# Three tile buffers, one x1 chunk buffer, and the final 1x1 in four whole chunks, in a two-layer convolution kernel on one Trainium2 core

## The reference, cut to what matters

```python
# layer 0; gn is group normalisation with 32 groups of 16 channels
g   = gn(x)
f   = relu(einsum('oc,nchw->nohw', Wc, g) + bc)              # 512 -> 128 channels, 1x1
gk1 = relu(mean(g, axis=(2, 3)) @ Wc.T + bc)                  # gate from the means
xm  = g.reshape(N, C, 3, H // 3, 3, W // 3).max(axis=(3, 5))  # 3x3 grid of maxima
sk  = relu(einsum('oc,nckl->nokl', Wc, xm) + bc)
dynW = relu(Wck applied to (gk1 * Wkk + bkk, sk) + bck)       # a 3x3 kernel of its own for each image
y   = conv3x3(f, dynW) + b_ad                                 # 128 -> 128 channels
x1  = x + einsum('oc,nchw->nohw', Wf, y) + bf                 # the final 1x1, 128 -> 512 channels
# layer 1
out = x1 + conv3x3_grouped(gn(x1), kernels, groups=32)        # 16 -> 16 channels in each group
```

## Time and profile before

| | us |
|---|---|
| median of 3 runs | 4146.16 |
| the profiled execution, its own time | 4137.59 |
| its span | 4135.8 |
| mean granted clock of TensorE | 0.953 |

### The profile page before, as it was taken

How to read it: one execution, slowest core, us unless ns; L and a number is a source line. 1 busy time by engine, 2 the same in 40 slices (tenths; PEclk the granted TensorE clock), 3 DMA queues, 4 the chain that set the end, 5 groups by cost and what they waited for, 6 DMA issues and landing times.

```text
span 4135.8 us, 60434 instructions
## 1 busy us (share of the span) xinstructions
PE 3670.0 (89%) x18688; PEld 2884.0 (70%) x18688; DVE 2569.5 (62%) x5557; ACT 2126.7 (51%) x3559; POOL 960.6 (23%) x1036
## 2 busy tenths in 40 slices
PE   4798998899998889998889988899988899888996
PEld 3676777667777667777667766677766677766774
DVE  5766666666666666666566656666666666666642
ACT  3355555555554555545555555655445555555554
POOL 2022222222212222122222222222222222222223
PEclk9899999999999999999999999999999999999997
DMA  4465655765656756656756557656567566576555
GB/s 91 139 186 154 173 155 148 189 174 162 169 144 153 200 159 167 170 139 168 187 154 171 153 142 196 170 166 163 149 155 191 157 166 166 141 183 179 146 150 123
DMA packets 317590, 666.98 MB, mean 161 GB/s; under 512 B 58863, under 2 KB 288242, under 8 KB 288645
## 3 DMA queue, kind: packets, MB, share of 16 engines
q1 hardware_dynamic: 317317, 663.34, 61.0%
HBM read 355.00 MB, written 308.28 MB: 160 GB/s over the span
## 4 chain that ended last, share of the span: by engine, by line
issue 65%; POOL 20%; PE 9%; DVE 2%; DMA 2%; ACT 1%; POOLq 1%; SPq 0%; DVEq 0%; ACTq 0%
POOL hl L408 19%; PE pb L858 1%; PE pb L860 1%; PE pb L859 1%; DMA big<-x_rows 1%; PE pac L858 1%; POOLq L407 1%; PE pd L858 1%; PE pd L859 1%; PE pd L860 1%; PE pac L859 1%; PE pac L860 1%; DMA out<-big 1%; DVE big L779 1%; DVE x1b L769 0%
## 5 line engine op out<-in xcount | busy, mean ns | idle before, releaser
L408 POOL TENSOR_TENSOR hl<-un,hl 128x384 f16<-128x384 f32 x1024 | 933.2, 911 | 3094.2 <-ACT hl L433 3094.0
L429 ACT ACTIVATE un<-big,b_t,s_t 128x384 f32<-128x384 f32 x1024 | 710.8, 694 | 455.2 <-DMA big<-x_rows 455.2
L858 PE MATMUL pd<-hl,k_h 128*96 128x384 f16 x1536 | 541.1, 352 | 234.9 <-POOL hl L408 234.9
L433 ACT ACTIVATE hl<-un 128x384 f16<-128x384 f32 x1024 | 538.9, 526 | 275.3 <-PE pb L860 183.9
L779 DVE SCALAR_TENSOR_TENSOR big<-pd,kout,big 96x768 f32<-96x768 f32 x256 | 259.2, 1012 | 539.5 <-PE pd L860 539.5
L858 PE MATMUL pb<-fh,dynh 128*128 128x480 f32 (+1 forms) x1440 | 549.6, 382 | 23.8 <-DVE xs L755 23.8
L860 PE MATMUL pb<-fh,dynl 128*128 128x480 f32 (+1 forms) x1440 | 546.5, 379 | 0.0
L859 PE MATMUL pb<-fl,dynh 128*128 128x480 f32 (+1 forms) x1440 | 545.2, 379 | 0.0
L859 PE MATMUL pd<-hl,k_h 128*96 128x384 f16 x1536 | 537.1, 350 | 0.0
L860 PE MATMUL pd<-hl,k_l 128*96 128x384 f16 x1536 | 536.9, 350 | 0.0
L443 ACT ACTIVATE xs<-big,negm 128x480 fp32r<-128x480 f32 (+1 forms) x640 | 401.0, 671 | 227.1 <-PE pac L860 225.0
(11 more groups left out here) (114 smaller groups left out, 5505.0 us busy)
## 6 DMA issues: line engine op xcount, KB each, us to landing
big<-x SPq DMA_DIRECT2D x128, 1152.0 KB, 9.9
x_rows<-x1b SPq DMA_DIRECT2D x128, 1152.0 KB, 6.6
big<-x_rows SPq DMA_DIRECT2D x128, 1152.0 KB, 9.5
out<-big SPq DMA_DIRECT2D x128, 1152.0 KB, 6.4
big<-x_rows SPq DMA_DIRECT2D x256, 192.0 KB, 10.8
x_rows<-mrow SPq DMA_DIRECT2D x64, 96.0 KB, 1.9
big<-kt SPq DMA_DIRECT2D x4, 288.0 KB, 10.8
big<-kt SPq DMA_DIRECT2D x2, 192.0 KB, 11.8
```

Of the source, the lines that this page charges most:

```text
L408: pool.tensor_tensor(hl[:, g % HL_RING, 1, :, 1:W + 1], un[:, g % U_RING], hl[:, g % HL_RING, 0, :, 1:W + 1], ALU.subtract).then_inc(hl_lo, 1)
L429: act.activation(un[:, g % U_RING], t_slot(g // GQ)[:, g % GQ], ACT.Identity, bias=b_t[:, g:g + 1], scale=s_t[:, g:g + 1]).then_inc(u_done, 1)
L433: act.activation(hl[:, g % HL_RING, 0, :, 1:W + 1], un[:, g % U_RING], ACT.Copy).then_inc(hl_hi, 1)
L858: pe.matmul(acc, high_w, high_x, start=start, stop=False)
```

## The change

There are three tile buffers, so chunks 0, 1 and 2 have one each and chunk 3 follows chunk 0. There is one chunk buffer for x1, so chunk c may be filled when chunk c-1 is written and squared. The final 1x1 has a whole chunk of six units in each of rounds 0, 4, 8 and 11. The group means of x1, and their transfers, move from stage D into the next step, between stages A and B; all tile loads stand behind them. The squares and some statistics move to other rounds. Image 1's loads no longer wait for `k_lo`; step 1's `write_means` does.

```diff
-X1_SLOTS = 2
-T_SLOTS = 2
-T_SLOT = [0, 1, 0, 1]
+X1_SLOTS = 1
+T_SLOTS = 3
+T_SLOT = [0, 1, 2, 0]
-C_ROUNDS = 6
-C_PER_ROUND = CUNITS // C_ROUNDS
+C_AT = {0: 0, 4: 1, 8: 2, 11: 3}
-SQUARE_AFTER = {7: 0, 10: 1, 13: 2, 16: 3}
-ROOT_AFTER = 24
-GATES_AFTER = 30
+SQUARE_AFTER = {6: 0, 14: 1, 22: 2, 28: 3}
+ROOT_AFTER = 23
+GATES_AFTER = 28
...
                     sp.wait_ge(max_done, Q)
-                    sp.wait_ge(k_lo, K_PARTS)
...
                 if T_SLOT[c] in T_SLOT[:c]:
                     sp.wait_ge(stored[T_SLOT.index(T_SLOT[c])], written)
                 else:
-                    reached(sp, stored[Q - 1 - T_SLOT[::-1].index(T_SLOT[c])], free)
+                    sp.wait_ge(stored[Q - 1 if c == 0 else c], written)
...
                 if k == 0:
-                    if c < X1_SLOTS:
-                        reached(vec, x1_out[c + X1_SLOTS], n * 16)
-                        reached(vec, sq_done, n * Q)
+                    if c == 0:
+                        reached(vec, x1_out[Q - 1], n * 16)
                     else:
-                        vec.wait_ge(x1_out[c - X1_SLOTS], (n + 1) * 16)
-                        vec.wait_ge(sq_done, n * Q + c - X1_SLOTS + 1)
+                        vec.wait_ge(x1_out[c - 1], (n + 1) * 16)
+                    reached(vec, sq_done, n * Q + c)
...
                 if d:
+                    x1_group_means(n - 1)
                     x1_variances(n - 1)
```

More of the change, by code:

```diff
@@ L68 @@
 PREP_MEANS_AT = 6
+GROUP_MEAN_AFTER = 7
 PREP_VARIANCES_AT = 8
[L70 to L73, removed]
 GROUP_VARIANCE_AFTER = 9
-KERNEL_INPUTS_AFTER = 12
-KERNELS_AFTER = 14
-X_HIGH_AFTER = {26: (0, 1), 28: (2, 3), 30: (4,)}
+PREP_SCALED_AT = 10
+KERNEL_INPUTS_AFTER = 11
+KERNELS_AFTER = 13
+X1_SUMS_AT = 12
+X_HIGH_AFTER = {28: (0, 1), 30: (2, 3), 31: (4,)}
 X_LOW_AT = {13: (0, 1), 14: (2, 3), 15: (4,)}
@@ L304, in load_t @@
             def load_t(n, c):
-                written, free = (n + 1) * 16, n * 16
+                written = (n + 1) * 16
                 above, below = partition_of(0), partition_of(IR - 1)
@@ L333, in step @@
                     store(n - 2, Q - 1)
+                if more:
+                    load_x(n + 1, 1 - odd, 2)
+                    load_x(n + 1, 1 - odd, 3)
                 if d:
@@ L336, in step @@
                         sp.wait_ge(k_lo, K_PARTS)
[L337 to L343, removed]
+                    write_means(n - 1)
+                    for c in range(Q - 1):
+                        load_t(n - 1, c)
                 write_x1(n, 0)
@@ L376, in _ @@
             store(N - 2, Q - 1)
-            for c in range(2):
+            write_means(N - 1)
+            for c in range(Q - 1):
                 load_t(N - 1, c)
[L379 to L382, removed]
+            store(N - 1, 0)
+            load_t(N - 1, Q - 1)
+            for c in range(1, Q):
                 store(N - 1, c)
             for c in range(Q):
-                sp.wait_ge(stored[c], N * 16)
+                sp.wait_ge(stored[c], (N + 1 if c else N) * 16)
         @block.gpsimd
@@ L390, in _ @@
             pool.memset(stage, 0.0).then_inc(bands_zero, 1)
+            for c in range(1, Q):
+                pool.memset(token[:, c:c + 1], 0.0).then_inc(stored[c], 16)
             pool.memset(ind[:, :, :], 1.0).then_inc(pool_const, 1)
@@ L803, in step @@
                         output(n - 1, r)
-                    if r < C_ROUNDS:
-                        for u in range(r * C_PER_ROUND, (r + 1) * C_PER_ROUND):
+                    if r in C_AT:
+                        for u in range(C_AT[r] * OR_, (C_AT[r] + 1) * OR_):
                             residual(n, odd, u)
@@ L818, in step @@
                         x1_means(n)
-                    if r == X1_MEANS_AT:
-                        x1_group_means(n, more)
                     if more:
@@ L846, in _ @@
             images(vec, step)
+            x1_group_means(N - 1)
             x1_variances(N - 1)
@@ L923, in kernel_inputs @@
                     pe.matmul(acc, cent[:, c, :], wcs[:, c, :], start=c == 0, stop=False)
-                pe.matmul(acc, f32(onesr[0:1, 0:GATES]), bcr[0:1, :], start=False, stop=True).then_inc(stat_mm, 1)
+                pe.matmul(acc, f32(onesr[32:33, 0:GATES]), gates[32:33, :], start=False, stop=True).then_inc(stat_mm, 1)
             def dyn_kernels(n):
@@ L959, in step @@
                         d_pair(n - 1, r)
-                    if r < C_ROUNDS:
-                        for u in range(r * C_PER_ROUND, (r + 1) * C_PER_ROUND):
+                    if r in C_AT:
+                        for u in range(C_AT[r] * OR_, (C_AT[r] + 1) * OR_):
                             c_unit(n, u)
-                    if r == GROUP_VARIANCE_AFTER:
+                    if r == PAIRS - 1:
                         x1_group_means(n)
```

21 lines of the change are left out of this document (9 added, 12 removed).

## The result

The changed kernel takes 3792.81 us (median of 4 runs, 3790.61 to 3798.21). The kernel before took 4145.38 in the same comparison; the ratio is 0.9158, with a 95% interval from 0.9133 to 0.9183. The profiled execution of the changed kernel took 3793.06, its span is 3791.3. Against the 4137.59 and 4135.8 of before that is 344.5 less, where the prediction had 375.

A forecast was written before the change was run, and what follows sets the result against it. TensorE was taken as the bound, losing time in stage D to late tile loads and low clock. Sums of 360 and 391 gave a middle of 375: 4137.6 - 375 = 3763, stated as 3765; 8 in 10 from 3712 to 3860.

The forecast's parts named there:

- likeliest case: Whole kernel: the forecast itself, a time of 3715 to 3830 us, chance 0.74.
- first sum: Full steps: waits 7.0, clock 3.1, means 0.5, final 1x1 0.7 make 11.3, less 0.5; 360 with both ends.
- new timetable: Stage D and start of B: issue and landing times; tile load 3 lands at 33 to 35, six us to spare.
- Squares: Stage D, ScalarE, after groups 6, 14, 22 and 28: groups behind them ready 0.5 to 0.9 early; 0.2 us taken.
- rival 1: Stage D: ScalarE late behind its squares, each a us late; 5.5 lost a stage, time 3935, chance 0.11.
- rival 3: Stage D: tile load 3 stays late, half of the loss stays; 5.3 a stage, time 3929, chance 0.04.
- single chunk buffer: Stage D: a single write takes 5.6 us where 12.0 and 9.2 are available; wait taken as 0.
- Step 0: First image: 26 gained against 17.7 for three waits for a write, partly hidden; bounds 8 and 26, 18 taken.
- the 26: Step 0: TensorE's wait of 23.81 for x of image 1 goes and its clock is kept, 26 us gained.
- second count: Stage D counted up from its parts: 65.3, 12.3 less than 77.6; less 0.5, with 25.5 for the ends, 391.
- stage A: Start of each step: 15.2 us, counted as filled, with no change foreseen.
- The last step and the last image: End of run: a stage D's 11.3 - 0.5, and 10.5 less some 3 us for the first tile load, 7.5.

The follow-up runs named there:

- e2: Changed kernel with two tile buffers instead of three, loads 2 and 3 queued behind the writes of chunks 1 and 2: 4293.44 us, ratio 1.0375.
- e7: Against the two-tile-buffer kernel e2: tile load 3 moved ahead of the write of chunk 2 in SyncE's queue: 4121.26 us, ratio 0.9954.
- e3: Changed kernel with chunk 1 of the final 1x1 moved from round 4 to round 1, next to chunk 0: 3908.23 us, ratio 0.944.
- e4: Changed kernel with one scaling of the next image's 1x1 weights moved from round 10 to 11, its small products to round 12: 3752.66 us, ratio 0.9067.
- e5: Changed kernel with the low part of the next image's dynamic kernels made before round 15's output on VectorE: 3663.38 us, ratio 0.8851.
- e10: Changed kernel with the loop over images ended two images earlier and these two steps written out behind it: 3793.83 us, ratio 0.9163.
- e8: The changed kernel measured a second time, unchanged: 3797.18 us, ratio 0.9176.

## Why the prediction was right, and where it was off

The forecast of 3765 stood 28 us below the measured 3792.8, within the likeliest case's own range. Step by step:

- **Stage D, right to 0.1 us, in part by luck (see below).** The first sum had 11.3 - 0.5 = 10.8 less per stage, measured are 77.75 - 66.96 = 10.79. All the waits it counted went, and the clock with them. How the 10.8 divide is partly shown: without the third buffer, in the best order tried, stage D is 73.74, so the third buffer brings 6.8 and the rest of the change 4.0.
- **The new timetable, right.** Write of chunk 0 at 7.6 (7.6 measured), of chunk 1 at 22.9 (22.9), of chunk 2 at 38.3 (38.5), tile load 3 at 23.7 (23.5), a round with units 6.5 long (6.49). The means left 1.7 us after the start of B (1.7), tile load 0 4.4 (4.7 foreseen), and ScalarE took its first group 19.2 after the start of B without a wait. Tile load 3 is the exception: it was to land 33 to 35 after the start of D, and in the median of steps 3 to 28 its large part came at 34.3 and its last small part at 37.1, since the large part took 10.8 and not the 8.8 of the earlier trace rows. Of the six us to spare four were left.
- **Squares, right.** TensorE waits for GpSimd in no full step; rival 1 did not occur. Nor did rival 3; what it would have cost shows in e2 against e7, where a tile load 3 that ScalarE waits 9.5 for costs stage D 4.7 (5.3 were put on it).
- **The single chunk buffer, right in full steps.** VectorE waits for no write of x1.
- **Step 0, right in size and wrong in mechanism.** The net is 19.6 where 18 were foreseen. But the prediction took the loss against the 26 to be three waits for a write, and VectorE waits for none: the 8.0 that step 0 got longer behind stage B begin with the 8.32 for x's chunk 0. That wait covers the write's; in e3, where chunk 1 comes ahead of the statistics, VectorE waits 5.64 for the write in step 0, and step 1 starts 2.1 us earlier all the same. The Trainium skill ("Trainium Kernel Development and Optimization", Best Practices) asks for double-buffering so that transfers overlap with compute. By e3 the rule holds where chunks follow each other (4.8 us of stage D). The prediction said that the trace agrees for step 0, and the trace of before does show VectorE waiting 2.48 and 0.45 for writes there; in the changed kernel statistics and a load stand between chunks 0 and 1, and no such wait is left.
- **A term that was left out: the scaling in round 10.** The prediction's second count came to 65.3 for stage D, and measured was 66.96. Of these 1.7, 1.3 are the scaling of the weights, which the change moves from round 11 to round 10, ahead of a round with units, and which I did not cost at all; it is TensorE's wait of 1.32 in round 11, a wait over 1 us in stage D of the kind that the prediction said should not occur. e4 shows it: 30 such waits are 39, and e4 is 40 faster. The rest is a slip in the sum: a round's six units add 3.52, four rounds 14.1, and 47.4 + 14.1 + 4.2 is 65.6 and not 65.3; e4's stage D has 65.68. The trace of before has the scaling at 282 ns each, and here it takes 508 (2.03 / 4), beside a busy GpSimd (last section). Without that slowing, 1.2 us for the four, output 11 would have been late by some 0.1 only (estimate from these durations and from e4's 1.27). With the scaling put in, the second count, 391, becomes 351.
- **A term taken as constant: stage A.** The prediction let A stand at 15.2. It was 15.62 in the mean, and took 13.62 to 16.46 from step to step, where before nearly every step had 15.2. That is the clock after the 3.1 us wait, as e5 shows: with the wait down to 0.76 stage A takes 13.62 in each of steps 2 to 29. It costs some 30 x 0.4 = 12 against the forecast. Why the loss depends on the step is open.
- **Step 30.** 7.5 us behind the loop, shown by e10 to belong to leaving it. It was not in any row of before, where the same step was 2.6 shorter than the mean.
- **The last step and the last image** gave 21.9 where 10.8 + 7.5 = 18.3 were foreseen. The 3 us that were put on the first tile load, for the means and chunk 3's store ahead of it, came to 0.4: TensorE waits 18.35 there, and 17.97 before.

The 15.5 us between the first sum (360) and the 344.5 measured are mostly stage A with 12 and step 30 with 7.5; the first and the last image were better than foreseen by 5. The 1.3 of the scaling are not among them, because an error of the other sign hid them: without it a stage would have gained 12.1 and not 10.8, which is what the second count said (12.3, or 12.0 without its slip). The first count, made from printed waits, was too small by about what the scaling took; that the two met at 0.1 us is luck.

## What to carry to other kernels

When a buffer is short, look first at what stands ahead of its load in the issuing queue: here two places in SyncE's order moved the time by 295 us with the same buffers and bytes, and the third buffer by 205. A single buffer cost nothing where the work between a transfer's start and the next use was longer than the transfer (here 10 to 12 us against 5.6), so the place of the use can pay for the memory of another buffer. A short wait of TensorE at a stage's border can cost nearly twice its length through the clock (2.33 off the wait brought 4.33), so an operation moved ahead on another engine, as in e5, can give more than its own time.

## What was not expected of the hardware

**VectorE slows beside GpSimd.** In step 0 the changed kernel makes the same four scalings at the same place in round 10, but has no tiles of an image before it, and GpSimd's timeline is empty from 95.8 to 150. There they take 0.87 us instead of 2.03, and the product of two 128x4 tiles on line 593 takes 0.16 instead of 0.53:
```profile
129.16 0.16 DVE L593 TENSOR_TENSOR va<-va 128x4 f32<-128x4 f32 x1
...
129.75 0.87 DVE L654 TENSOR_SCALAR wcs<-wc,va 128x128 f32<-128x128 f32 x4
```
In the steps after it line 593 takes 526 to 529 ns each of 30 times, and the scalings up to 917 ns each:
```profile
L593 DVE TENSOR_TENSOR va<-va x30: 526/528/529, 235.4 to 3582.8; 128x4 f32<-128x4 f32 x30
L654 DVE TENSOR_SCALAR wcs<-wc,va x120: 273/540/917, 236.4 to 3584.8; 128x128 f32<-128x128 f32 x120
```
GpSimd makes a low part every 1.15 us beside them. In e4 the scalings fall into a gap of GpSimd and take 0.87 again; there GpSimd's next low part lies beside VectorE's subtraction of two tiles and takes 1.31 instead of 0.89, so either engine can pay:
```profile
1721.73 1.31 POOL L405 TENSOR_TENSOR hl<-un,hl 128x384 f16<-128x384 f32 x1 [3.32 <-ACT hl L430]
```
ScalarE is not the cause: in the kernel before nearly all scalings lie beside its operations and all away from GpSimd's, and take 278 to 289 ns each. That VectorE and GpSimd hold each other up is shown by these places; by what mechanism is not. The Trainium skill ("GPSIMD Engine Reference", Specifications) gives one: GpSimd's path to SBUF is shared with VectorE, and contended by VectorE's operations that read two inputs there or run in a mode with two ports. The product and the subtraction have two inputs, and the trace agrees; for the scaling, which has one large input, it would mean such a mode, which no row shows.

**The clock's loss after the same wait of 3.09 us varies** between 0 and 2.8 us from step to step, while stages B and D are the same to 0.05. In the changed kernel stage A takes 13.6 (no loss) in steps 3, 4 and 31, and from step 8 on it goes through 14.9, 15.2, 16.3, 16.4 and 16.5 again and again; in e8, the same kernel, the cycle is there from step 9 on.
